# The order of loads in the two attention stages of a four-layer kernel

## The reference, cut to what matters

```
# layer 2 (relative attention), x already normalized, y = context
q = x @ Wq + bq;  k = y @ Wk + bk;  v = y @ Wv + bv
content = (q + r_w_bias) . k            # per head
rel     = relative_shift((q + r_r_bias) . pe)
attn    = (content + rel) / sqrt(16)
attn    = attn * mask - 1e10 * (1 - mask)
out     = softmax(attn) @ v @ Wo + bo
# layer 3: the same without rel and mask
```

## Time and profile before

| | us |
|---|---|
| median of 3 runs (lowest, highest) | 2017.14 (2012.15, 2019.18) |
| the profiled execution | 2025.68 |
| its span, first to last instruction | 2023.8 |
| layer-2 attention | about 1104 to 1494 of the span |
| layer-3 attention | about 1592 to 1787 |
| mean granted TensorE clock | 0.825 of 2.4 GHz |
| busy share of the span: PE, DVE, ACT, POOL | 70%, 62%, 28%, 17% |

### The profile page before, as it was taken

One profiled execution on the slowest core, in us unless ns is written; L12 is line 12 of the kernel. 1 busy time (PEld: TensorE's weight loads), 2 busy tenths in 40 slices (PEclk: granted clock), 3 DMA queues, 4 the chain that ended last, 5 costly groups with the idle time before them and its releaser, 6 DMA issues. The chain is left out here.

```text
span 2023.8 us, 32390 instructions
## 1 busy us (share of the span) xinstructions
PE 1415.0 (70%) x9677; PEld 1190.1 (59%) x9677; DVE 1244.7 (62%) x3152; ACT 575.9 (28%) x1634; POOL 335.4 (17%) x474
## 2 busy tenths in 40 slices
PE   4659999999999660000034666666769899959998
PEld 2338888888888550000011455555658699948887
DVE  5866767676767476956676455444644366655555
ACT  2322121212121130000000344444535377723322
POOL 4740000000000010000011223222321011132221
PEclk9679999999999855555555677777879899979999
DMA  5532121212121242032342344444422111100000
GB/s 179 178 116 48 27 52 27 52 27 52 27 52 27 69 125 34 0 63 42 90 146 72 96 118 112 122 114 122 114 66 72 51 45 52 42 16 17 21 21 16
DMA packets 176316, 137.64 MB, mean 68 GB/s; under 512 B 16818, under 2 KB 170243, under 8 KB 173892
## 3 DMA queue, kind: packets, MB, share of 16 engines
q1 hardware_dynamic: 158864, 119.75, 22.7%
q10 hardware_dynamic: 17396, 17.23, 3.0%
HBM read 100.87 MB, written 36.06 MB: 68 GB/s over the span
## 5 line engine op out<-in xcount | busy, mean ns | idle before, releaser
L704 DVE TENSOR_TENSOR moa_oe<-moa_mask,moa_ogT 128x1024 fp32r<-128x1024 bf16 x128 | 155.4, 1224 | 36.9 <-PE moa_k_ps L93 33.8
L91 PE MATMUL moa_k_ps<-moa_w_out_hi,moa_oe 128*128 128x256 f32 x512 | 150.8, 294 | 13.5 <-DVE moa_oe L704 13.5
L1126 PE MATMUL warp_t_ps<-ident,warp_entry 128*128 128x128 f32 x1 | 0.5, 475 | 221.2 <-DVE warpb_hit L1109 221.2
L1831 PE MATMUL L_r_ps<-ident,L_prob 128*128 128x128 f32 x512 | 81.1, 295 | 101.8 <-ACT L_prob L1659 101.7
L1841 PE MATMUL L_b_ps<-L_v,L_pT 128*128 128x128 f32 x1024 | 145.8, 307 | 1.4 <-DVE L_xo L1527 0.8
L1841 PEld LDWEIGHTS L_b_ps<-L_v,L_pT 128*128 128x128 f32 x1024 | 140.6, 222 | 6.8 <-issue 6.8
L92 PE MATMUL moa_k_ps<-moa_w_out_lo,moa_oe 128*128 128x256 f32 x512 | 144.3, 282 | 0.0
L93 PE MATMUL moa_k_ps<-moa_w_out_hi,moa_oe 128*128 128x256 f32 x512 | 144.1, 281 | 0.0
L1126 PEld LDWEIGHTS warp_t_ps<-ident,warp_entry 128*128 128x128 f32 x1 | 0.2, 182 | 221.5 <-DVE warpb_hit L1109 221.5
L1831 PEld LDWEIGHTS L_r_ps<-ident,L_prob 128*128 128x128 f32 x512 | 63.6, 150 | 110.8 <-ACT L_prob L1659 105.8
L1659 ACT ACTIVATE L_prob<-L_att,L_nmax 128x128 f32<-128x128 f32 x256 | 81.4, 395 | 115.2 <-DVE L_nmax L1555 115.2
(11 more groups left out here) (334 smaller groups left out, 3776.9 us busy)
## 6 DMA issues: line engine op xcount, KB each, us to landing
bounce<-L_rel SPq DMA_DIRECT2D x64, 258.0 KB, 4.5
moa_mask<-chosen SPq DMA_DIRECT2D x32, 512.0 KB, 5.8
L_shifted<-bounce SPq DMA_DIRECT2D x64, 256.0 KB, 3.7
ret_staged_values<-in_w_value_dram ACTq DMA_DIRECT2D x8, 512.0 KB, 3.8
ret_staged_outputs<-in_w_out_dram ACTq DMA_DIRECT2D x8, 512.0 KB, 3.9
ret_cT<-in_ctxT_pairs_dram SPq DMA_DIRECT2D x16, 256.0 KB, 2.8
L_x<-x_after SPq DMA_DIRECT2D x32, 128.0 KB, 2.3
L_cT<-in_ctxT_pairs_dram SPq DMA_DIRECT2D x32, 128.0 KB, 2.4
```

The costliest lines, as they stand in the source:

```text
L91: pe.matmul(out, x_hi, w_hi, start=first, stop=False)
L704: dve.tensor_tensor(oe[e % 2][:, :, :, :].rearrange("p a m s -> p a (m s)"), mask[:, e, :, :].rearrange("p m s -> p (m s)").unsqueeze(1).t ...
L1126: pe.transpose(t_ps[:, 0:128], entry[:, :], k.ident[:, :]).then_inc(entry_T, 1)
L1831: last = pe.transpose(r_ps[g % 2][:, j, :], prob[:, 4 * g + j, :], k.ident[:, :])
```

## The change

In SP's step, x of batch b+4 (not b+3) is loaded first of all, into the buffer that batch b+2 leaves. Then come the store and the residual as before, then in layer 2 all four table writes, one wait until DVE has done all four adds of batch b+1, the context of b+3, the four reads and last the mask of b+2. ACT's copy of a group into `rel` no longer waits for the add. In layer 3 the context keeps its wait for the value projection. As a last x is now loaded one step earlier, `in_deep_phases` unrolls two more steps for every engine of these two stages; what the other engines do in a step, and in which order, stays.

```diff
+def in_deep_phases(engine, step):
+    step(-1, 1, middle=False, tail=False)
+    step(0, 0, tail=False)
+    with engine.Fori(0, (B - 6) // 2) as i:
+        step(i * 2 + 1, 1)
+        step(i * 2 + 2, 0)
+    step(B - 5, 1)
+    step(B - 4, 0)
     step(B - 3, 1)
...
                 def step(b, u, ahead=True, front=True, middle=True, tail=True):
                     nu = 1 - u
-                    more = not isinstance(b, int) or -2 < b < B - 3
-                    b_less = not isinstance(b, int) or b + 2 < B
+                    if ahead and (not isinstance(b, int) or b + 4 < B):
+                        sp.wait_ge(ln.xn_ready, after(b + 3))
+                        load_x(b + 4, u)
                     if tail:
                         sp.wait_ge(xo_ready, after(b))
                         sp.dma_start(x_out[b - 1], xo[nu][:, :]).then_inc(x_stored[nu], 16)
                         if not isinstance(b, int) or b + 1 < B:
                             load_residual(b + 1, nu)
-                    if ahead and more:
-                        sp.wait_ge(ln.xn_ready, after(b + 2))
-                        load_x(b + 3, nu)
-                        sp.wait_ge(v_done, after(b + 2))
+                    if ahead and relative:
+                        for r in range(4):
+                            write_group(b, u, r)
+                    if ahead and (not isinstance(b, int) or -2 < b < B - 3):
+                        if relative:
+                            sp.wait_ge(att_ready, after(b * 4 + 8))
+                        else:
+                            sp.wait_ge(v_done, after(b + 2))
                         load_context(b + 3, nu)
-                    if middle and relative and b_less:
+                    elif ahead and relative:
+                        sp.wait_ge(att_ready, after(b * 4 + 8))
+                    if ahead and relative:
+                        for r in range(4):
+                            read_group(b, u, r)
+                    if middle and relative and (not isinstance(b, int) or b + 2 < B):
                         sp.wait_ge(masked_ready, after(b * 4 + 4))
                         load_mask(b + 2, u)
-                    if ahead and relative:
-                        write_group(b, u, 0)
-                        write_group(b, u, 1)
-                        write_group(b, u, 2)
-                        read_group(b, u, 0)
-                        write_group(b, u, 3)
-                        read_group(b, u, 1)
-                        read_group(b, u, 2)
-                        read_group(b, u, 3)
...
-                        act.wait_ge(att_ready, after(b * 4 + (r + 5)))
                         act.activation(rel[:, 4 * r:4 * r + 4, 1:S + 1], r_ps[r % 2][:, :, :], ACT.Copy).then_inc(rel_out, 1)
```

More of the change, by code:

```diff
@@ L103, in in_three_phases @@
         step(i * 2 + 2, 0)
+    step(B - 3, 1)
+    step(B - 2, 0, ahead=False)
+    step(B - 1, 1, ahead=False, front=False)
+    step(B, 0, ahead=False, front=False, middle=False)
+def in_deep_phases(engine, step):
[6 more added lines that the diff above has]
+    step(B - 4, 0)
     step(B - 3, 1)
@@ L1434, in step @@
                             load_residual(b + 1, nu)
-                    if ahead and more:
-                        sp.wait_ge(ln.xn_ready, after(b + 2))
-                        load_x(b + 3, nu)
-                        sp.wait_ge(v_done, after(b + 2))
-                        load_context(b + 3, nu)
-                    if middle and relative and b_less:
+                    if ahead and relative:
[6 more added lines that the diff above has]
+                            sp.wait_ge(v_done, after(b + 2))
+                        load_context(b + 3, nu)
+                    elif ahead and relative:
[4 more added lines that the diff above has]
+                    if middle and relative and (not isinstance(b, int) or b + 2 < B):
                         sp.wait_ge(masked_ready, after(b * 4 + 4))
                         load_mask(b + 2, u)
-                    if ahead and relative:
-                        write_group(b, u, 0)
-                        write_group(b, u, 1)
-                        write_group(b, u, 2)
-                        read_group(b, u, 0)
-                        write_group(b, u, 3)
-                        read_group(b, u, 1)
-                        read_group(b, u, 2)
-                        read_group(b, u, 3)
                 step(-2, 0, front=False, middle=False, tail=False)
-                in_three_phases(sp, step)
+                in_deep_phases(sp, step)
                 for u in range(2):
@@ L1485, in _ @@
                 pool.wait_ge(setup, after(n_setup))
-                in_three_phases(pool, step)
+                in_deep_phases(pool, step)
             @block.vector
@@ L1648, in _ @@
                     dve.tensor_scalar(q_bias[:, :], bq[:, :], SCALE, None, ALU.mult).then_inc(setup, 1)
-                in_three_phases(dve, step)
+                in_deep_phases(dve, step)
             @block.scalar
@@ L1751, in _ @@
                 step(-2, 0, front=False, middle=False, tail=False)
-                in_three_phases(act, step)
+                in_deep_phases(act, step)
             @block.tensor
@@ L1923, in _ @@
                 step(-2, 0, front=False, middle=False, tail=False)
-                in_three_phases(pe, step)
+                in_deep_phases(pe, step)
 FF, RANK = 1024, 64
```

## The result

The changed kernel takes 1955.78 us, the median of 4 runs (1952.02 to 1964.1); the kernel before took 2014.64 on the same chip (2010.28 to 2019.18). The ratio is 0.9701, with a 95% interval of 0.9678 to 0.9725: faster, by 3.0%. The forecast was 1945, with a range of 1922 to 1978. So the spans of the two profiles differ by 73.6 us where the medians differ by 58.9, and a sum over profiles must be held against the first of these numbers. In the listings of the changed kernel the lines stand 16 or 17 further down: mask_add is L1581, the statistics L214, the relative scores L1826, the transposes L1847, the context keys L1790.

A forecast was written before the change was run, and what follows sets the result against it. VectorE's wait for x, queued behind the table's writes and reads, bound layer 2. Thirteen periods of 18.1 us save 55.5, the first steps 16.5, together 72.0: 2025.68 becomes 1953.7, on the median 1945; range 1922 to 1978.

The forecast's parts named there:

- The place of the new wait: Layer 2, VectorE: the wait moves from the statistics of x to mask_add, some 13 mask waits of 4 to 5 us.
- The period: Layer-2 loop from mask_add through the fourth write, its landing, fourth read and mask: 18.1 us, ends 16.25 and 20.7.
- mask to mask_add: End of the layer-2 loop: the mask lands 2.3 us after its issue, plus 0.1 to reach VectorE.
- The sum: Layer 2: thirteen periods fall from 290.85 to 235.3 us, gaining 55.5; with 16.5 from the first steps, 72.0.
- The start-up term: First layer-2 steps: waits of 7.84 and 7.03 us go, the next step gains 5.8, less 4.1 for cold matmuls: 16.5.
- Were that cover gone: Layer 2, TensorE: a late context, if the mask wait no longer covered it, would cost up to 1 us a step.
- From profile to median: Whole kernel: the profiled 2025.68 us lay 8.5 above the median 2017.14; the sum 1953.7 becomes 1945 on the median.
- (b): Layer 2: the mask lands in time and the engines bind; period 14.3, gain 121.5, time 1896 us; chance 0.05.
- (c): Layer 2: the wait moves but the path stays as long; period 21.9, gain 22.7, time 1994 us; chance 0.08.
- (d): Layer 2: the four reads serialize ahead of the mask; slower, period 30.85, time 2111 us; chance 0.03.
- (e): Layer 2: no effect, VectorE waited for another transfer landing with x; time 2017 us; chance 0.02.
- The clock rule: TensorE in layer 2: a DMA wait every turn makes each step start cold; period 19.1, whole 1958 us.

## Why the prediction was right

**The place of the new wait: right.** DVE has no wait for x in the loop and 14 waits for the mask, 5.3 each (some 13 of 4 to 5 were forecast). The mask goes 0.62 after the fourth read, that read right at the landing of the fourth write. Moving the mask's issue by 1.78 us moved the time in its direction by more than that; moving it ahead of the table removed the wait. So the loop is shown, not only argued.

**The period: right to 0.1 us, by its parts nearly so.** Forecast 18.1, measured 17.99. In the step shown, from mask_add to the fourth write it took 8.7 (8.95 forecast at the full clock), the landing 5.1 (5.0), the mask's issue 0.6 (0.7), mask to mask_add 3.1 (2.4). This last term was undersized: the landings of the masks have a median of 3.0 behind the reads, where they had 2.5 ahead of the table. The overrun is made up by the clock: I took half of the cold steps' extra 2.05, and only four of 13 were cold, with periods of 18.2 to 19.1 beside 17.0 to 17.5 for most of the others.

**The sum: right to a microsecond, with an error inside.** 13 periods gave 57.0 where 55.5 was forecast, and the end of the stage 1.4. The start-up term was too high: 12.6 measured for 16.5. That these errors nearly cancel is luck. The first two waits gave 7.9 and 5.5 (7.84 and 7.03 forecast, before 4.1 for cold matmuls). But the step that ends at mask_add of batch 2 gained nothing: 22.59 us before, 23.44 after, where I had written "gains 5.8 like the rest". Even a period of 18.1 would have gained only 4.5 there, since this step took 22.59 and not 23.9. Mask 1 is already in its buffer, so DVE does not wait at mask_add, and the work of PE that elsewhere fits into that wait comes behind it: the keys and queries (L1790) start 3.4 after mask_add, where in the steady step they start 3.5 before it. The fourth write and the mask also land a microsecond later than there (6.1 and 4.0). Nor does anything cover the late context. PE waits at 1143:

```profile
1143.16 1.16 PE L1790 MATMUL L_a_ps<-L_xnT,L_wq 128*128 128x128 f32 x8 [1.85 <-DMA L_cT<-in_ctxT_pairs_dram]
...
1147.36 1.14 PE L1826 MATMUL L_r_ps<-L_pz,L_qrT 32*128 32x256 f32 x8
```

and the writes of the table start only at 1149.15, the mask at 1159.20, 19.4 after mask_add instead of 14.45 (1252.17 - 1237.72). The late context is only a part of this: with the context early and the mask last the same step takes 20.57 us, 2.9 less than here, and still 2.5 more than the forecast period. The prediction named the price of a late context under "Were that cover gone", and set it at up to 1 us a step. It is more: some 1.4 us a step at full clock, by the kernels with the mask early or not loaded, and 2.7 with the steps at the lower clock that came with it.

**From profile to median.** Layer 2 took 384.99 us and takes 313.97, from its first statistics to its last xo: 71.0, for 72.0 forecast. The other 2.6 of the profiles' 73.6 lie outside it. The medians differ by 58.9, since the profile of before fell 11 above the median of its runs there. The kernel with layer 3 alone changed shows where such microseconds lie: its layer 2 is that of before, its profiled execution took 2018.79 us, 6.9 less than the profiled one of before, and its 13 periods took 284.65, 6.2 less. In this pair, then, what one execution took longer than the other lies almost wholly in the loop whose wait for x the change takes away. The sum took 72 from such an execution, which came out within 2 us (1953.7 forecast, 1952.02 measured), and then from the median too. That is the likely reason why 1945 is 11 us too low; it rests on this one pair, and how the loop ran in a median execution no trace shows.

**The rivals.** (b), the compute-bound period of 14.3, did not come: the mask's place excludes it, and both runs that issue mask and context ahead of the table, as before, fall to 13.5. (c) and (d) have tails that were not seen; four reads in a row take 4.29 us to issue and overlap, so they don't serialize. (e) is excluded by the first line of the waits. Layer 3 gave 0, as forecast, and SyncE's single wait for the adds held nothing that shows. ScalarE's wait was priced at the 0.21 us that it held before; put back into the new order it holds 0.53.

**The clock rule.** By the Trainium skill (TensorE: Matmul & The Clock Gate, HAM oscillation) a DMA wait inside the loop can throttle the array again in every turn. The trace agrees in four of 13 turns of the changed kernel, with PE idle 2.5 to 3.3 us before them, and not in nine, idle 1.9 to 2.6. It agrees in twelve of 13 of the kernel with the mask later, idle 3.1 to 4.7. With every step cold the forecast had T = 19.1 and a time of 1958. The median of 1955.78 lies near it, but that is luck: the measured period is 17.99.

## What to carry to other kernels

When a load is moved ahead in a queue, ask of every load that it passes what its distance to its use was, and whether it can spare it: here x needed to be further ahead, mask and context lost the slack that they had, and the part of the change that nobody needed cost more than was left of the gain. Try the parts apart before the whole is kept. A wait that is covered by a longer one is not free; it is the next bound, and it is uncovered wherever the longer wait is missing, as in the first steps of a loop.

## What the runs showed of the hardware

Taking one wait away from TensorE made it slower elsewhere: with the context early its idle time for mask_add and the copy behind it grew from 2.6 to 3.75 us a step (36.5 and 52.5 us in 14 waits), the steps at a low clock from four to nine of 13, and in such a step 16 matmuls took 2.97 us instead of 1.95. The same idle time is not answered the same way each time: 2.51, 2.58 and 2.97 us were followed by a granted clock of 0.72 in the next 6 us, 2.47 and 2.59 by 1.00. Shorter waits were answered both ways too: in the kernel without mask loads a wait of 1.54 us for the context was followed by 1.00 over the next 4 us, one of 1.57 by 0.57. A mask of 64 KB lands in 3.0 us behind four reads of 256 KB, and in 2.5 in its old place (medians): these reads hold it up by half a microsecond, not by their own length. Four such reads, issued in 4.3 us, were no slower for the kernel than the old mixture of reads and writes: 0.2 points between the two orders.
